# Projections: line rows in the last two row banks, an earlier first value copy, and no fp32 copy of the rows

## What is computed

```
qkv = x @ qkv_w + qkv_b                       # q, k, v: 16 heads of 16
w1, w2 = x_prev @ w1_write, x @ w2_write      # 16 heads of 4 numbers
r1, r2 = x @ w1_read, x @ w2_read
def exterior(p1, p2):                         # 6 numbers per head, divided by their length
    L = stack([p1[i] * p2[j] - p1[j] * p2[i] for i, j in _PAIRS4])
    return L / max(sqrt(sum(L * L)), 1e-12)
write_lines, read_lines = exterior(w1, w2), exterior(r1, r2)
J_write = write_lines @ _J6                   # reversed, two of the six with a minus
geo_v, gate = x @ geo_w + geo_b, sigmoid(x @ gate_w + gate_b)
std_logits = q . k * 16 ** -0.5
geo_logits = read_lines . J_write * inc_scale
```

## Time and profile before

| | |
|---|---|
| median of 3 runs (lowest to highest) | 1736.34 us (1735.85 to 1738.46) |
| the profiled execution: time, and span in the trace | 1734.03 us, 1732.3 us |
| PE, ACT, DVE, POOL busy | 1604.8, 1223.8, 1073.9, 336.5 us |
| first transfer of the second stage | 228.87 us after the start of the span |

### The profile page before, as it was taken

The page is one execution under the profiler, slowest core; times in us unless marked ns, Lnnn a source line. Parts: engine busy times, 40 slices in busy tenths (PEclk is TensorE's granted clock), DMA queues, the critical chain, the costliest instruction groups (busy, mean ns, idle before and its releaser), DMA issues. The chain is left out here.

```text
span 1732.3 us, 31799 instructions
## 1 busy us (share of the span) xinstructions
PE 1604.8 (93%) x11809; PEld 561.6 (32%) x11809; DVE 1073.9 (62%) x2621; ACT 1223.8 (71%) x1457; POOL 336.5 (19%) x479
## 2 busy tenths in 40 slices
PE   7988456999999999999999999999999989999997
PEld 4544211222222222222222222222222225555564
DVE  4776475676676776667667676677676424544333
ACT  3554314998999999999998999999999952221211
POOL 4333131122121211211202112021121232211000
PEclk9999756999999999999999999999999999999999
DMA  5665521212212122121121211212213024222000
GB/s 166 210 204 185 176 90 66 90 48 85 89 52 73 49 69 73 50 71 61 59 83 51 71 66 55 72 49 69 73 43 128 20 73 132 81 73 85 12 12 25
DMA packets 95580, 140.31 MB, mean 81 GB/s; under 512 B 6353, under 2 KB 64529, under 8 KB 93361
## 3 DMA queue, kind: packets, MB, share of 16 engines
q1 hardware_dynamic: 94208, 135.08, 23.5%
q0 software_dynamic: 624, 2.75, 0.6%
q10 hardware_dynamic: 576, 0.28, 0.1%
HBM read 81.96 MB, written 55.61 MB: 79 GB/s over the span
## 5 line engine op out<-in xcount | busy, mean ns | idle before, releaser
L1218 ACT ACTIVATE prob<-ex 128x1024 f32<-128x1024 f32 (+1 forms) x1152 | 1055.3, 975 | 128.6 <-PE ex L1037 111.7
L1237 DVE TENSOR_REDUCE mp<-mx 128x1 f32<-128x512 f32 x768 | 492.8, 685 | 203.5 <-PE mx L1075 203.5
L1132 PE MATMUL pv<-prob,va 128*32 128x512 f32 (+3 forms) x5120 | 588.6, 541 | 1.8 <-POOL prob L1005 0.4
L1005 POOL TENSOR_SCALAR_AFFINE_SELECT prob<-prob 128x256 f32<-128x256 f32 (+1 forms) x384 | 186.2, 485 | 966.7 <-ACT prob L1218 962.0
L1043 PE MATMUL ex<-dq,dk 34*128 34x512 bf16 (+7 forms) x2560 | 335.8, 348 | 7.9 <-ACT prob L1218 2.2
L1234 DVE CUSTOM_DVE_ANT_0 dull<-mx,mask_qk 128x128 f32<-128x128 f32 (+3 forms) x512 | 223.2, 487 | 97.0 <-PE mx L1075 96.9
L1075 PE MATMUL mx<-dk,dq 64*128 64x512 bf16 (+3 forms) x1280 | 227.4, 356 | 19.8 <-issue 12.4
L1037 PE MATMUL ex<-gq,gk 38*128 38x512 bf16 (+3 forms) x1280 | 218.8, 355 | 10.8 <-DMA dq<-mrow 9.1
L1037 PEld LDWEIGHTS ex<-gq,gk 38*128 38x128 bf16 x1280 | 56.5, 93 | 418.9 <-ACT prob L1218 363.9
L1132 PEld LDWEIGHTS pv<-prob,va 128*32 128x32 f32 x5120 | 108.5, 108 | 232.8 <-issue 187.2
L1561 ACT ACTIVATE sg<-pg 128x512 f32<-128x512 f32 x48 | 28.7, 597 | 219.1 <-PE pg L1501 219.0
(11 more groups left out here) (109 smaller groups left out, 902.2 us busy)
## 6 DMA issues: line engine op xcount, KB each, us to landing
values<-vn SPq DMA_DIRECT2D x32, 512.0 KB, 5.2
va<-values SPq DMA_DIRECT2D x16, 1024.0 KB, 18.0
raw<-on SPq DMA_DIRECT2D x64, 256.0 KB
parts_dot<-sp SPq DMA_DIRECT2D x32, 384.0 KB, 5.0
dq<-parts_dot SPq DMA_DIRECT2D x96, 128.0 KB
dk<-parts_dot SPq DMA_DIRECT2D x96, 128.0 KB
parts_geo<-sp SPq DMA_DIRECT2D x16, 288.0 KB, 2.9
gq<-parts_geo SPq DMA_DIRECT2D x96, 48.0 KB
```

The source lines that it names most:

```text
L1005: g.affine_select(out=cut, in_=cut, compare_op=ALU.is_ge, fill=0.0, base=0, pattern=[[0, nb], [1, P]], channel_multiplier=-1).then_inc(mas ...
L1132: last = pe.matmul(pv[blk * VW:(blk + 1) * VW, CH - w:CH], sets[which]["v"][:, kb, blk * VW:(blk + 1) * VW], prob[UNIT_AT[s, j, kind] % NP ...
L1218: act.activation(prob[n % NPROB][:, :].rearrange("p (b c) -> p b c", b=2)[:, :, 0:w], ex[:, n % 2, :].rearrange("p (b c) -> p b c", b=2)[: ...
L1237: return v.tensor_reduce(out=to, in_=source, axis=AX.X, op=ALU.max)
```

## The change

- Row blocks 4 and 5 go to banks 2 and 3 in place of 0 and 1. PE's `qk_rows` of blocks 0 and 1 no longer wait for them; blocks 2 and 3 do.
- `t32` and its ScalarE copy are gone (48 instructions). VectorE forms the rest from the PSUM bank itself, with the bias added in the same instruction, and a bank is now free when VectorE's rest is done (`d_done`) in place of ScalarE's two reads. The q scale of 1/4 that ScalarE applied is multiplied into `w_qk` once at the start (`scaled`, which PE waits for).
- The value copy of the next chunk's tile 0 moves up in VectorE's order, from behind the line chain to between `ss` and `rn`. Value copies wait for the value matmuls alone (`nv_ready`), no longer for the whole tile (`n_ready`).
- The six multiplications that wrote the reversed write lines, and `rinc` and `rneg`, are replaced by two instructions on 384 elements: `lead` (lines times reciprocal length) and one with `signed` (sign times inc_scale), which is made once at the start.

```diff
-    LN_WRITES = 1 + NCOMP
-    LINKS = 7
+    LN_WRITES = 2
+    LINKS = 6
...
+    BANK = (0, 1, 2, 3, 2, 3)
@@ token_tiles
-                        pe.matmul(bank[:, 0, :], xc[par][:, k, tok], wv[:, k, :], start=k == 0, stop=k == NK - 1)
+                        last = pe.matmul(bank[:, 0, :], xc[par][:, k, tok], wv[:, k, :], start=k == 0,
+                                         stop=k == NK - 1)
+                    last.then_inc(nv_ready, 1)
@@ qk_rows
-                        pe.wait_ge(row_act, ((c - 1) * NR + m + (5 if m < NR - 4 else 1)) * 2)
+                        pe.wait_ge(d_done, (c - 1) * NR + (m if m < 2 else m + 2) + 1)
@@ line_rows
-                    pe.wait_ge(row_act, (c * NR + m - 3) * 2)
+                    pe.wait_ge(d_done, c * NR + m - 1)
...
-                        last = pe.transpose(pr[m % 4][0:ROWS[m], tt * P:(tt + 1) * P],
+                        last = pe.transpose(pr[BANK[m]][0:ROWS[m], tt * P:(tt + 1) * P],
@@ row_in
-                act.activation(t32[m][0:n, :], pr[m % 4][0:n, :], ACT.Identity, bias=bias, scale=scale)\
+                act.activation(sp3[m][0:n, SLOTS[m][0], :], pr[BANK[m]][0:n, :], ACT.Identity, bias=bias)\
                    .then_inc(row_act, 1)
-                act.activation(sp3[m][0:n, SLOTS[m][0], :], pr[m % 4][0:n, :], ACT.Identity, bias=bias,
-                               scale=scale).then_inc(row_act, 1)
@@ vector, once
+            v.tensor_scalar(wqk[:, :, 0:D], wqk[:, :, 0:D], SCALE_Q, None, ALU.mult).then_inc(scaled, 1)
+            for i in range(NCOMP):
+                last = v.tensor_scalar(signed[:, :, i], incb[:, :], float(J_SIGN[i]), None, ALU.mult)
+            last.then_inc(dve, 1)
@@ first_rest
-                v.tensor_tensor(out=d32[m][0:n, :], in0=t32[m][0:n, :], in1=sp3[m][0:n, SLOTS[m][0], :],
-                                op=ALU.subtract).then_inc(d_done, 1)
+                if m < 4:
+                    v.scalar_tensor_tensor(out=d32[m][:, :], in0=pr[BANK[m]][:, :], scalar=bqs[:, m:m + 1],
+                                           in1=sp3[m][:, SLOTS[m][0], :], op0=ALU.add, op1=ALU.subtract)\
+                     .then_inc(d_done, 1)
+                else:
+                    v.tensor_tensor(out=d32[m][0:n, :], in0=pr[BANK[m]][0:n, :], in1=sp3[m][0:n, SLOTS[m][0], :],
+                                    op=ALU.subtract).then_inc(d_done, 1)
@@ chunk
-                    v.wait_ge(n_ready, c * TT + tt + 1)
...
+                    if head or tt:
+                        value_tile(c, tt, head)
...
                 v.tensor_scalar(ss[:, :], sum6[:, :], 1e-24, None, ALU.max).then_inc(ss_ready, 1)
+                if more:
+                    value_tile(c + 1, 0, False)
                 v.wait_ge(nrm_ready, c + 1)
```

More of the change, by code:

```diff
@@ L442, in project @@
         rn = sb("rn", [P, TT, 2, H])
-        rinc = sb("rinc", [P, TT, H])
-        rneg = sb("rneg", [P, TT, H])
+        lead = sb("lead", [P, TT, H, NCOMP])
+        signed = sb("signed", [P, H, NCOMP])
         most = sb("most", [P, 1])
         ln = sb("ln", [P, TT, 2, H, NCOMP])
-        t32 = [sb(f"t32_{i}", [P, CH]) for i in range(NR)]
         d32 = [sb(f"d32_{i}", [P, CH]) for i in range(NR)]
@@ L455, in project @@
         n_ready = sem("n_ready")
+        nv_ready = sem("nv_ready")
+        scaled = sem("scaled")
         v_out = sem("v_out")
@@ L629, in _ @@
             token_tiles(0, 0, 1, True)
+            pe.wait_ge(scaled, 1)
             qk_rows(0, 0, True)
@@ L653, in row_in @@
                 bias = bqs[:, m:m + 1] if m < 4 else 0.0
-                scale = SCALE_Q if m < 2 else 1.0
                 act.wait_ge(rows_ready, c * NR + m + 1)
@@ L674, in points @@
                 if tt == 0 and not head:
-                    act.wait_ge(dve, (c - 1) * LINKS + 4)
+                    act.wait_ge(dve, (c - 1) * LINKS + 5)
                 bank = pn[tt % 2][:, 1, :]
@@ L729, in first_rest @@
             def first_rest(c, m, head):
-                v.wait_ge(row_act, (c * NR + m + 1) * 2)
+                v.wait_ge(row_act, c * NR + m + 1)
                 if not head:
@@ L735, in first_rest, with value_tile, chunk @@
                 n = ROWS[m]
-                v.tensor_tensor(out=d32[m][0:n, :], in0=t32[m][0:n, :], in1=sp3[m][0:n, SLOTS[m][0], :],
-                                op=ALU.subtract).then_inc(d_done, 1)
-            def chunk(c, head, second):
-                base = c * LINKS + 3
-                for tt in range(TT):
-                    v.wait_ge(n_ready, c * TT + tt + 1)
[L743 to L749, removed]
+                if m < 4:
[5 more added lines that the diff above has]
+                                    op=ALU.subtract).then_inc(d_done, 1)
+            def value_tile(c, tt, head):
+                v.wait_ge(nv_ready, c * TT + tt + 1)
+                if not head:
+                    v.wait_ge(v_st[tt], c * 16)
+                v.tensor_tensor(out=vn[tt][:, :, 0:DH],
+                                in0=pn[tt % 2][:, 0, :].rearrange("p (h d) -> p h d", d=DH),
+                                in1=bv[:, :].rearrange("p (h d) -> p h d", d=DH),
+                                op=ALU.add).then_inc(v_out, 1)
+            def chunk(c, head, second, more):
+                base = c * LINKS + 4
+                for tt in range(TT):
+                    if head or tt:
+                        value_tile(c, tt, head)
                     if not head:
@@ L784, in chunk @@
                 v.wait_ge(dve, base + 5)
[L785 to L790, removed]
+                v.tensor_tensor(out=lead[:, :, :, :], in0=line_v[:, :, 1, :, :],
+                                in1=rn[:, :, 1, :].unsqueeze(3).to_broadcast([P, TT, H, NCOMP]),
+                                op=ALU.mult).then_inc(dve, 1)
                 if not head:
@@ L797, in chunk @@
                     op=ALU.mult).then_inc(ln_ready, 1)
[L798 to L806, removed]
+                v.wait_ge(dve, base + 6)
+                v.tensor_tensor(out=ln[:, :, 0, :, ::-1], in0=lead[:, :, :, :],
+                                in1=signed[:, :, :].unsqueeze(1).to_broadcast([P, TT, H, NCOMP]),
+                                op=ALU.mult).then_inc(ln_ready, 1)
+            chunk(0, True, False, True)
+            chunk(1, False, True, True)
+            with v.Fori(2, NC - 1) as c:
+                chunk(c, False, False, True)
+            chunk(NC - 1, False, False, False)
             for m in range(NR):
```

## The result

| | before | changed |
|---|---|---|
| median (lowest to highest) | 1737.40 us (1735.85 to 1738.48, 4 runs) | 1714.56 us (1713.80 to 1715.90, 4 runs) |
| ratio, 95% interval | | 0.987 (0.9853 to 0.9887) |
| profiled execution: time, span | 1734.03, 1732.3 us | 1713.80, 1712.1 us |
| second stage's first load | 228.87 us | 210.24 us |

The change gains 1.3%.

The account below looks back on a forecast made before the run. PE, with some 3.3 us of waits per chunk, bounds chunks 1 to 5, two-engine operand loads chunks 6 and 7. 16.9 + 0.6 + 0.7 = 18.2 off 1736.34 gives 1718.1 us; own range 1715 to 1720.5, eight in ten 1713.5 to 1725.

Parts of the forecast that it names:

- Chunks: Chunks 1 to 5: without PE's two waits each takes 19.5 us, where it took 22.8.
- the schedule named above: Times within a chunk from its first tile's start T, such as value copy at T+10.5, block 3's rest ending T+11.8.
- The margin of 0.2 at the second transposes: PE's second four transposes start at T+12.0, 0.2 us after the rest of row block 3 ends, so no wait.
- that of ScalarE before the root: Row block 3's store holds ScalarE until T+20.8, which the root can bear up to T+22.2.
- The rival of new waits on PE: Chunks 1 to 5 get new PE waits, chance 0.20: 1723.1 us at 1 us per chunk, 1728.8 if 2.13 returned.
- the 16.3: Five chunks of 19.5 start chunk 6 16.3 us earlier: 10.65 from the banks, the rest value-copy waits and one slow pass.
- five times 2.13: PE's 2.13 us wait between transposes and row matmuls goes in five chunks through the bank move: 10.65 us.
- The step that the 48 reads are hidden except at the end: Dropping ScalarE's fp32 copy saves only one bank read after the last landing: 0.58 us, taken as 0.6.
- The rest from PSUM: VectorE's rest read from PSUM takes 0.69 us against 0.68 from SBUF, so it costs nothing.
- Load phase: Operand loads on two engines start 16.9 us earlier and still take 59 us, so their end moves by 16.9.
- the dry queue: Rival, chance 0.08: the load queue runs dry and SP's order sets the end; gain 20.1 us, 1716.2.
- The tail: After the last landing 0.6 and 0.7 us saved; GpSimd's six take 8.5, second stage starts 3.5 behind their end.

Follow-up runs that it names:

- a_split: Changed kernel with each of the 24 operand loads issued as two; 1694.09 us, ratio 0.9753 to the kernel before.
- a_early: Changed kernel with the operand loads unsplit but issued one chunk earlier in SP's order; 1715.38 us, ratio 0.9878 to the kernel before.
- a_fp32: Changed kernel with the fp32 copy (`t32`) kept and the rest formed from SBUF; 1717.08 us, ratio 0.9891 to the kernel before.
- a_split_early: Changed kernel with the operand loads both split in two and issued one chunk earlier; 1695.56 us, ratio 0.9764 to the kernel before.
- b_banks: Kernel before with only the bank move (line rows in banks 2 and 3); 1740.24 us, ratio 1.0029 to the kernel before.
- b_copy: Kernel before with only the early value copy and `nv_ready`; 1725.65 us, ratio 0.9936 to the kernel before.
- a_old_banks: Changed kernel with the line rows back in banks 0 and 1; 1721.88 us, ratio 0.9917 to the kernel before.
- b_split: Kernel before with each of the 24 operand loads issued as two; 1718.00 us, ratio 0.9897 to the kernel before.

## Why the prediction was right, and where it was not

**Chunks.** Right: 19.28 for a forecast of 19.5, and every time of the schedule named above within 0.1. The margin of 0.2 at the second transposes held: the eight take 1.10 in place of 1.04. So did that of ScalarE before the root, by 0.16 in the closest chunk. The rival of new waits on PE did not come.

**Where the 16.3 comes from.** Wrong. The prediction wrote 10.65 of it to the bank move, five times 2.13. Alone that move loses 6.7 us in `project`. The waits were not separate prices: PE, ScalarE and VectorE run in a ring, each waiting in turn for the one before, and what is taken from one wait turns up in the other until the value copy is moved as well. With the rest of the change in place the move is worth 7.0. The sum held because the change does both.

**No fp32 copy.** The step that the 48 reads are hidden except at the end holds with the new chain in place, nearly: 0.6 was forecast and 1.8 measured in `project`, some 1.0 of it one chunk's wait. With the old chain it fails: with it a chunk takes 19.32 without the reads and 20.04 with them.

**The rest from PSUM.** 0.74 with the bias pointer, 0.69 for the 96-row form; 0.69 was taken. The Trainium skill's page (VectorE: DVE Perf Modes, the section on the TRN2 errata) gives an estimate of 0.065 more than from SBUF: the trace agrees for the four with the pointer (0.74 against 0.68 in the earlier trace rows), and not for the 96-row rests or the value copies. The four are also of another instruction form, so the 0.06 may be the form's; no run separates the two.

**Load phase.** Right: it starts 17.4 earlier (16.9 forecast) and keeps its length, 59.14; the dry queue did not come. That the length is that of loads on few engines was argued in the prediction and is borne out by a_split.

**The tail.** The path from the last landing to the first rest went from 4.59 to 196.78 - 193.46 = 3.32, 1.3 shorter as forecast. Behind that the step was wrong in its parts and right in its sum, by luck: GpSimd's six took 6.71 in place of 8.53, and the second stage's first load came 5.3 behind GpSimd's end in place of 3.5, so it is 12.0 behind GpSimd's start in both kernels (228.87 - 216.85, 210.24 - 198.26). The end of the stage in GpSimd's timeline, of before, the changed kernel and a_early:

```profile
228.87 0.21 POOL L965 MEMSET negm<- 128x128 f32 x1 [3.49 <-POOLq L413]
210.24 0.21 POOL L981 MEMSET negm<- 128x128 f32 x1 [5.26 <-POOLq L414]
211.22 0.21 POOL L978 MEMSET negm<- 128x128 f32 x1 [3.56 <-POOLq L414]
```

Before, GpSimd's end plus 3.5 is the rule, and it is in a_fp32 too (200.57 + 8.38 + 3.42). In the changed kernel the landings of the last stores end the stage later. The load of `va` is issued at 193.32, ahead of the last six stores:

```profile
va<-values SPq DMA_DIRECT2D x1, 1024.0 KB, 10.9
```

It lands 10.9 later, at 204.2, when five of the six stores have been issued (before, at 221.6, it was two), and all six land behind it, 4.7 to 5.7 after their issue where those of before took 2.5 to 3.6. In a_early and a_split_early that load is issued 25 to 27 us before them, GpSimd takes 6.72, they land 2.6 to 3.0 after their issue, and the first load comes 3.5 to 3.6 behind GpSimd's end again: 10.2 to 10.3 behind its start in place of 12.0.

**The size.** The second stage's first load was forecast at 210.7 and came at 210.24. Measured from chunk 1's start the gain is 19.5 for 18.2 forecast, since chunk 1 began 0.9 later than before; that start lay between 27.98 and 29.68 in all kernels, with and without the work added at the start, and is no cost that can be told. The medians are 22.8 apart, 3.3 more than the stage gives; 1.1 of that is the median of before, 1737.40 from four runs where the forecast had 1736.34 from three. The interval, 19.6 to 25.5 us, starts about at the 19.5; behind that first load the profiled executions take 1501.2 to 1506.2 us without a pattern, and nothing in them was found that the change would shorten. This difference stays open.

## What to carry to other kernels

Waits of one engine for others are not prices to add up: where engines run in a ring, remove one and read whether the chunk got shorter, for the same time may come back at the next wait, and as one long standstill at a lower clock. Work that is "hidden" is hidden by a margin that several edits share: the copy and the long chain were each nearly free and together cost 6.5 us. A stretch in which the transfer share falls to 0.12 again and again and never below, and which keeps its length when its start moves, was here a queue of loads on few engines; splitting them was worth nearly as much as the whole change (19.0 beside 19.5 in `project`). And a time that stays equal, like the 12.0 at the end of the stage, can have two different causes: look at what ended it in both kernels.

## What the runs showed of the hardware

- After a standstill of 3.1 in b_banks PE's clock was granted at 0.58 over the next 2.6 us. After waits of 1.15 to 1.48, in b_copy and a_old_banks, no row pass was slow (7.14 each); after 2.13, before and in b_split, it was 7.14 or 8.84.
- At the end of the stage GpSimd's six subtractions took 8.38 to 8.53 beside rests for which VectorE reads both inputs from SBUF, and 6.71 to 6.72 beside rests with one input from PSUM.
- In the steady chunks of the changed kernel the transfers already move 182 to 300 GB/s in windows of 10 us from 39 to 129 us, at a share of 0.57 to 1.00; with the loads spread, in a_split, the share went to 0.97 at 264 GB/s from 135 to 145 us, and issuing the loads a chunk earlier gained nothing.
